# A convolutional attention block with a mixture of experts: z stored in partition order, its tables laid out ahead, and k's spreading transfers issued by SyncE

## The reference

```python
xn = ln_over_channels(x)                       # eps 1e-6
for s in (0, 2):                               # SHIFTS: once plain, once rolled by (-2, -2)
    xs = roll(xn, -s)
    for half in (xs[:, :32], xs[:, 32:]):      # 8 heads of 4 channels, windows of 4x4 pixels
        q, k, v = split(qkv_w @ half)          # qkv_w is 96 x 32
        lepe = depthwise_conv3x3(v, lepe_w)
        o = softmax(q @ k.T * 4 ** -0.5 + bias) @ v + lepe    # inside each window
    result += roll(o, s)
x = x + result
t = tokens(x)                                  # 9216 tokens of 64 for each image
tn = ln(t)                                     # eps 1e-5
p = softmax(tn @ router_w + router_b)          # 8 experts, the best 2 are kept and renormalised
t = t + sum_over_best_2(p_e * (tn @ expert_w[e] + expert_b[e]))
```

## Time and profile before

| | us |
|---|---|
| median of three runs | 3744.56 |
| lowest and highest run | 3741.43, 3759.62 |
| time of the profiled execution | 3730.37 |
| its span, first to last instruction | 3728.5 |

### The profile page before, as it was taken

One profiled execution on the slowest core, in us unless ns is written; L12 is line 12 of the kernel. 1 busy time (PEld: TensorE's weight loads), 2 busy tenths in 40 slices (PEclk: granted clock), 3 DMA queues, 4 the chain that ended last, 5 costly groups with the idle time before them and its releaser, 6 DMA issues.

```text
span 3728.5 us, 203806 instructions
## 1 busy us (share of the span) xinstructions
PE 3199.5 (86%) x82757; PEld 1956.7 (52%) x82757; DVE 3190.4 (86%) x6174; ACT 2233.5 (60%) x4514; POOL 2942.7 (79%) x5385
## 2 busy tenths in 40 slices
PE   3889989988898888898889888888889888989884
PEld 1655555555555555555555555555555555555541
DVE  2789989998999989998889988888889988889983
ACT  2676666666666656665566656665556666666640
POOL 3988878888888878887788878877788878788860
PEclk8999999999999999999899999999899989999996
DMA  1245455555455545555545555545455545455545
GB/s 27 60 97 126 117 123 121 129 120 122 118 127 121 124 109 129 115 127 115 120 110 127 122 117 121 125 111 122 113 120 125 124 115 123 114 116 126 125 104 126
DMA packets 415302, 432.05 MB, mean 116 GB/s; under 512 B 129984, under 2 KB 395888, under 8 KB 414320
## 3 DMA queue, kind: packets, MB, share of 16 engines
q1 hardware_dynamic: 248432, 304.94, 36.0%
q0 software_dynamic: 165888, 113.57, 12.9%
HBM read 245.79 MB, written 58.98 MB: 82 GB/s over the span
## 4 chain that ended last, share of the span: by engine, by line
PE 36%; SPq 23%; issue 15%; DVE 14%; DMA 5%; ACT 3%; POOL 2%; DVEq 0%; ACTq 0%; POOLq 0%
SPq L397 13%; PE bank L628 8%; PE bank L564 7%; DVE lepe L899 4%; SPq L429 4%; PE bank L549 3%; PE bank L641 3%; PE bank L584 2%; SPq L455 2%; DVE gx L887 2%; PE bank L633 2%; DMA gate_rows<-gateT 2%; DVE row_max L907 2%; DMA z<-fin 2%; PE bank L653 2%
## 5 line engine op out<-in xcount | busy, mean ns | idle before, releaser
L504 POOL DMA_DIRECT2D vx<-vt x3072 | 1561.7, 517 | 414.1 <-PE bank L633 403.3
L628 PEld LDWEIGHTS bank<-probT,vx 128*32 128x32 f32 x36864 | 824.6, 189 | 464.5 <-issue 452.8
L628 PE MATMUL bank<-probT,vx 128*32 128x16 f32 x36864 | 886.3, 234 | 159.2 <-issue 144.0
L493 POOL DMA_DIRECT2D kx<-k_sb x1536 | 741.0, 489 | 229.5 <-issue 102.8
L564 PEld LDWEIGHTS bank<-kx,qx 32*32 32x32 f32 x36864 | 584.9, 110 | 443.6 <-issue 441.3
L564 PE MATMUL bank<-kx,qx 32*32 32x64 f32 x36864 | 689.3, 223 | 133.3 <-issue 111.1
L899 DVE SCALAR_TENSOR_TENSOR lepe<-vpad,lepe_sb,lepe 128x384 f32<-128x384 f32 x960 | 673.5, 702 | 0.8 <-issue 0.8
L718 ACT ACTIVATE prob<-prob 128x512 f32<-128x512 f32 x576 | 367.4, 638 | 288.1 <-DVE prob L912 285.0
L887 DVE TENSOR_TENSOR gx<-gate_wide,yn_pair 128x768 f32<-128x768 f32 x384 | 397.4, 1036 | 112.9 <-PE bank L549 62.1
L523 POOL TENSOR_TENSOR lepe_p<-lepe_p,tap_sb 128x384 f32<-128x384 f32 x384 | 434.9, 1133 | 32.7 <-issue 11.3
L912 DVE TENSOR_TENSOR prob<-bank,row_max 128x512 f32<-128x512 f32 x576 | 398.4, 692 | 16.7
(11 more groups left out here) (87 smaller groups left out, 4517.8 us busy)
## 6 DMA issues: line engine op xcount, KB each, us to landing
gate_wide<-gate_rows SPq DMA_DIRECT2D x384, 384.0 KB
vx<-vt POOLq DMA_DIRECT2D x3072, 12.0 KB
kx<-k_sb POOLq DMA_DIRECT2D x1536, 24.0 KB
yn_pair<-yn POOLq DMA_DIRECT2D x384, 96.0 KB
z<-fin SPq DMA_DIRECT2D x1344, 24.0 KB
xs<-in_x SPq DMA_DIRECT2D x96, 192.0 KB
xt<-in_x SPq DMA_DIRECT2D x192, 96.0 KB
z0t<-z SPq DMA_DIRECT2D x192, 96.0 KB
```

Source lines behind the costliest of these rows:

```text
L493: pool.dma_start(kx[to + m:to + C:4, r % 2, m, :], k_sb[at + m:at + C:4, r % 2, :])\
L504: pool.dma_start(vx[to:to + TOK, r % 2, g * 8 + x:g * 8 + 8:2, odd, :], vt[at:at + TOK, r % 2, x::2, :, :].rearrange("p h n k -> p h (n k)"))\
L628: last = MM(bank_o[32 * c:32 * c + 32, at * TOK:(at + 1) * TOK], vx[:, kr % 2, :, at % 2, at // 2 * 4 + c], probT[:, kr % 2, at, c * TOK:( ...
```

## The change

- `z` has one row for each partition of `fin` in place of two images in channel order, so that a strip is stored by one transfer of 128 rows in place of 11. `load_tile` takes the order apart again: its z part has 8 transfers in place of 5, with rows in runs of 16. The columns of the weights are permuted to match (`product` reads them through `ba`), x is given a second time with its channels in the tile's order, and the output's channels are put back on the host.
- All weights, the bias and the constants come as one table laid out ahead, loaded by one transfer. The 56 loads of before and the copies by which DVE, PE and ACT formed the tables are gone.
- `spread_gates` issues two transfers for each product p, in the slots 4, 5, 0 and 1 of a tile, each with a semaphore of its own; before it was four transfers for all p at once.
- `spread_k` moves from POOL to SP.

```diff
-    take_logits=34, gates=36, gap_exp=37, turn_gates=38, pair_yn=38, store_gates=39, spread_gates=41,
+    take_logits=34, gates=36, gap_exp=37, turn_gates=38, pair_yn=38, store_gates=39, spread_gates=40,
...
+            sp.dma_start(table[:, :], tables).then_inc(table_loaded, 16)
...
             load_pair(0, 0)
+            sp.wait_ge(spread_cleared, N_SPREAD_CLEARED)
...
+                if st := s.strip("spread_k"):
+                    k, r = st
+                    wait_alone(sp, k_saved, k + 1)
+                    if s.later(r, 2):
+                        wait_alone(sp, score_made, (k - 1) * UNITS)
+                    for m in range(4):
+                        for at, to in ((0, C), (C, 0)):
+                            sp.dma_start(kx[to + m:to + C:4, r % 2, m, :], k_sb[at + m:at + C:4, r % 2, :])\
+                                .then_inc(k_spread[r % 2], 16)
...
-                    def put(roll, a, b, q0, q1, part):
-                        sp.dma_start(z_cols[roll][im][:, a, b, q0:q1, :, here]
-                                     .rearrange("b q y n -> q y (b n)"), fin[part:part + 2 * (q1 - q0), r % 2, :])\
-                            .then_inc(z_stored[r % 2], 16)
...
+                    sp.dma_start(z[bass.ds(s.image(r, STRIPS), 1)][:, :, here].rearrange("b c n -> c (b n)"),
+                                 fin[:, r % 2, :]).then_inc(z_stored[r % 2], 16)
...
+                    def put_z(dst, half, roll, c_to, c_from, n, at, row, rows):
+                        part = half * C + c_to * TOK
+                        sp.dma_start(dst[part:part + n * TOK, r % 2, at * W:(at + rows) * W],
+                                     z_of[roll][:, c_from:c_from + n, :, row * W:(row + rows) * W]
+                                     .rearrange("b c q n -> c q (b n)")).then_inc(tile_loaded[r % 2], 16)
+
+                    def put_rolled(half, at, row, rows):
+                        put_z(z2t, half, 1, 1, 0, 3, at, row, rows)
+                        put_z(z2t, half, 1, 0, 3, 1, at, row, rows)
                     for half in range(2):
+                        put_x(half)
+                        put_z(z0t, half, 0, 0, 0, 4, 0, t * (2 * SP) + half * SP, SP)
+
+                    put_rolled(0, 0, (t * (2 * SP) + H - ROLL) % H, ROLL)
+                    put_rolled(0, ROLL, t * (2 * SP), SP - ROLL)
+                    put_rolled(1, 0, t * (2 * SP) + SP - ROLL, SP)
...
-                if ti := s.tile("spread_gates"):
-                    k, r = ti
-                    wait_alone(sp, gate_stored[r % 2], (k // 2 + 1) * 16)
+                if (ti := s.in_tile("spread_gates")) and ti[2] < PAIRS:
+
+                    k, r, p = ti
+                    if p == 0:
+                        wait_alone(sp, gate_stored[r % 2], (k // 2 + 1) * 16)
                     if s.later(r, 1):
-                        wait_alone(sp, gx_made, k * PAIRS)
-                    by_expert = gate_rows[r % 2].rearrange("(f p e) n -> e f p n", f=2, e=2)
+                        wait_alone(sp, gx_made, (k - 1) * PAIRS + p + 1)
+                    by_expert = gate_rows[r % 2].rearrange("(f p e) n -> e p f n", f=2, e=2)
                     for odd in range(2):
-                        for half in range(2):
-                            sp.dma_start(gate_wide[odd * C:(odd + 1) * C, :, half, :],
-                                         by_expert[odd, half].unsqueeze(0).broadcast_to([C, PAIRS, SPX]))\
-                                .then_inc(gate_spread[r % 2], 16)
+                        sp.dma_start(gate_wide[odd * C:(odd + 1) * C, p, :, :],
+                                     by_expert[odd, p].unsqueeze(0).broadcast_to([C, 2, SPX]))\
+                            .then_inc(gate_spread[p], 16)
...
+                    dve.wait_ge(gate_spread[p], (k + 1) * (GATE_DMAS * 16))
                     if p == 0:
-                        dve.wait_ge(gate_spread[r % 2], (k // 2 + 1) * (GATE_DMAS * 16))
                         dve.wait_ge(yn_paired[r % 2], (k // 2 + 1) * 64)
```

More of the change, by code:

```diff
@@ new lines, in tile_channels, with lay_tables, put @@
+def tile_channels():
+    return [half * CH + h * HEADS + c * 2 + y for c in range(4) for h in range(HD) for half in range(2) for y in range(2)]
+def lay_tables(qkv_w, lepe_w, bias_table, router_w, router_b, expert_w, expert_b):
+    t = np.zeros((128, TABLE_COLS), np.float32)
+    def put(name, rows, col, value):
+        at, n = TABLE_AT[name]
+        t[:, at:at + n][rows, col] = value
+    for name, a in CONSTS.items():
+        put(name, slice(0, 128), slice(0, a.shape[1]), a)
+    for g in range(4):
+        roll, half = g // 2, g % 2
+        rows = slice(g * CH, (g + 1) * CH)
+        for h in range(HD):
+            for m in range(HEADS):
+                a, b, y = m // 4, m // 2 % 2, m % 2
+                for part, name in ((0, "wq"), (1, "wk")):
+                    put(name, rows, g * CH + a * 16 + h * 4 + m % 4, qkv_w[part * CH + h * HEADS + m])
+                here = (h - 1) % HD if roll and a and b else h
+                one = qkv_w[2 * CH + here * HEADS + m]
+                put("wv", rows, g * CH + h * 8 + y * 4 + b * 2 + a, one)
+                at = (a * 2 + b) * CH + roll * 16 + h * 4 + half * 2 + y
+                put("wo", rows, at, one)
+                put("taps", at, slice(0, 9), lepe_w[here * HEADS + m].reshape(9))
+    for g in range(4):
+        for a in range(2):
+            for i in range(TOK):
+                for m in range(4):
+                    for j in range(TOK):
+                        dr, dw = i // SP - j // SP + SP - 1, i % SP - j % SP + SP - 1
+                        put("bias", g * CH + a * TOK + i, m * TOK + j, bias_table[dr * (2 * SP - 1) + dw, a * 4 + m])
+    order = tile_channels()
+    for half in range(2):
+        rows = slice(half * C, (half + 1) * C)
+        put("router", rows, slice(half * E, (half + 1) * E), router_w[order])
+        for p in range(E // 2):
+            put("experts", rows, slice(p * C, (p + 1) * C), expert_w[2 * p + half][np.ix_(order, order)])
+        put("expert_bias", slice(half * E, (half + 1) * E), slice(half * C, (half + 1) * C), expert_b[:, order])
+        put("router_bias", slice(half * E, (half + 1) * E), 0, router_b)
+    return t
@@ L179, in metaformer_block @@
+def metaformer_block(nc, x, x_tile, tables, out):
     ctx = ExitStack()
@@ L321, in _ @@
         def _(sp):
[L322 to L341, removed]
-                for half in range(2):
[L343 to L354, removed]
-                        .then_inc(const_loaded, 16)
-                    sp.dma_start(ebias_sb[half * E:(half + 1) * E, rows], expert_b).then_inc(const_loaded, 16)
```

194 lines of the change are left out of this document (65 added, 129 removed).

## The result

The changed kernel took **3989.91 us** (median of four runs, 3981.11 to 3993.32). The kernel before, on the same chip, took 3742.99 (3718.65 to 3759.62). The ratio is 1.0662, 95% interval 1.06 to 1.0723: slower by 6.6%. The forecast was 3783 with a range up to 3930, so the time lies outside it. The profiled execution took 3992.08, its span is 3990.3.

The account below looks back on a forecast made before the run. Three close limits bound the kernel: SP, DVE and PE. A loop through the gates of p = 3 (38.35 us a tile against 37.46) adds 80 us, less 42 for setup: +38 on the median, 3783 us, range 3570 to 3930.

Parts of the forecast that it names:

- start and tail: Outside the tile loop: earlier first matmul saves 34 us, last tiles no longer waiting for four gate spreads 8 more.
- k's price: Each SBUF-to-SBUF k issue on SP taken at 0.64 us; eight transfers 5.2 us, ends 3.2 to 7.0.
- x issue to gates in use: From the first x load to gates of p = 3 landed, queued behind x on two engines: 9.55 us, 9.0 to 10.5.
- z's loads on four and three engines: New z loads would crowd few engines, leaving up to 2.5 us ahead of gates and k: 40.8 us a tile.
- The range for x's start: On SP's queue, x loads start 17.05 us after `fin`, 13.1 to 20.4 with all ends.
- The forecast's own case: Loop through the gates of p = 3 gives 37.5 to 39.5 us a tile, 3706 to 3886 us; chance 0.42.
- Engines or issues dearer: k issues at 0.88 us or z loads crowding few engines: up to 41 us a tile, 3950 to 4020; chance 0.15.
- Cheap issues: k transfers on SP cost 0.40 us with gap: tile 36.35 us, total 3603 us; chance 0.22.
- the loop never closes: Loads at 5.9 us, z landing in 2.2: gates of p = 3 don't delay DVE, 3550 us; chance 0.13.
- Nothing but the setup: PE and DVE pace all tiles at 37.5 us; only the 42 us are saved, 3703 us; chance 0.08.
- The pace of PE and DVE alone: If the gates' loop stays open, DVE and PE set the tile at 35.5 to 36 us; chance 0.13.
- The forecast's turning point: Gates of p = 3 arriving 26.2 us after `fin`: there the loop eats the 42 us saved elsewhere.

Follow-up runs that it names:

- e2: Changed kernel with the gates of p = 3 issued ahead of the k transfers and x loads, k still on SP: 3718.77 us, 0.9947 of the kernel before.
- e4: Changed kernel with all eight gate transfers in slot 5 of a tile, k still on SP: 3668.44 us, 0.9821 of the kernel before.
- e1: Changed kernel with k's eight transfers back on POOL, all else as changed: 3632.79 us, 0.9712 of the kernel before.
- e6: Changed kernel with k's transfers back on POOL and the gates of p = 3 issued ahead of the x loads: 3422.87 us, 0.9151 of the kernel before.
- e3: Changed kernel with the 62-row x loads split into 48 and 14 rows, two issues more: 3874.69 us, 1.0367 of the kernel before.
- e5: Changed kernel with z's rows interleaved by roll, stored by eight transfers of 16 rows in place of one: 4233.69 us, 1.1318 of the kernel before.
- e10: Changed kernel with four of k's eight transfers on SP and four on POOL: 3834.26 us, 1.0247 of the kernel before.
- b1: Kernel before with k's transfers moved to SP and nothing else changed: 4417.9 us, 1.1828 of the kernel before.

## Why the prediction was wrong

**The mechanism was right.** The profile has what the prediction named: a loop of one tile from `fin` over z's landing, SP's queue and the gates of p = 3 back to `fin`; a DVE wait once a tile at p = 3; SP waiting for `fin` with throughput to spare (479.1 us in 99 times); PE's share of the chain gone. 28.95 + 12.15 = 41.1 us of loop (medians) stand against the measured tile of 41.32. The two experiments that take the gates of p = 3 out of the queue (e2, e4) end DVE's wait, and the one that takes k out (e1) shortens it. The two other causes that were named before those runs fell with them: if k's own lateness were the cost, e2, where k is later, would have been slower than 3990; and had the lower granted clock been a cause of its own, none of the three was expected to move. What part the clock has in the product's way to the next `fin` (12.15 us, 11.32 in e6) was not separated.

**The step that failed is the length of that loop**, forecast 26.6 + 11.75 = 38.35. Its terms, forecast and measured (from the timelines of the changed kernel; means over 66 tiles, since means add up, here to the tile of 41.32 within 0.01):

```
term                              forecast  measured  difference
fin to the first tile load          3.0       2.66      -0.3
ten tile loads                      7.45      7.61      +0.2
gates of p = 2                      1.4       1.87      +0.5
eight k transfers                   5.2       6.18      +1.0
x issue to gates p = 3 in use       9.55     10.74      +1.2
product p = 3 to the next fin      11.75     12.26      +0.5
```

The whole way from `fin` to the product is 29.07, +2.5, with +0.5 behind it; the tile itself is 2.97 longer than forecast. The two terms that failed most are the way from x's issue to the gates in use and the price of k. Between the first and the last tile this made +319.4 us where +80 were forecast, 239 too few; start and tail gave 57.6 in place of 42. The sum against the profiled execution thus missed by 224 us (3992 against 3768). Against the medians it is 207, since the profiled execution of before lay 14 us under its median and that of after 2 above.

- *k's price.* A single issue on SP takes a median of 0.589 us, within the 0.64 that was taken:

```profile
L391 SPq DMA_DIRECT2D kx<-k_sb x1536: 486/589/1921, 23.1 to 3873.0; - x192
```

From the first k to the first x it is 6.07, so 0.76 a transfer. The 0.64 came from three issues in a row in the setup, when nothing else ran. Longer single issues (up to 1.9; one of 1.32 in the tile shown) and the semaphore instructions ahead of the x loads are in the 0.76.
- *x issue to gates in use* was the term least known: it was built from shares of engines, with ends of 9.0 and 10.5, and measured just above the upper. e3 shows that its largest part, the wait behind x's 62-row loads on two engines, was right in kind: 3.3 of the 6.3 us of landing go when x is divided otherwise. Its parts were not right: x was to have landed 1.5 + 5.25 = 6.75 us after its issue and the gates 2.3 + 0.5 behind it; by the updates x lands after 9.7 and the gates 0.9 later. The 5.25 came from the start of the program, where nothing else moved. The Trainium skill (DMA: Bandwidth & Descriptors, Why a DMA increments its semaphore by 16 and not by 1; the prediction names another section of that page) says that a transfer is divided over the largest number of engines up to 16 that divides the slowest dimension of both sides. The runs agree: a set of x loads makes 28 updates with 62 rows and 84 with 48 and 14, and the ten tile loads the 102 named under e5. These counts fit 2, 16, 14, 4 and 3 engines, if a transfer on fewer than 16 counts one update more.
- *z's loads on four and three engines*, the mechanism weighed against the trace, given up to 2.5 us: e5 puts it near 1.0. The forecast was right to leave it out: the transfers did run on so few engines, and it costs little, since 7.5 us of issue go by meanwhile. (The 5.4 us of that passage is 5.5 by its own numbers, 98 KB against 93 in 5.25.)
- *Errors that add up.* Five of six terms were too small and one too large by 0.3. The range for x's start, 13.1 to 20.4 (its terms as stated reach 3.0 + 8.4 + 1.4 + 7.0 = 19.8), held the median of 18.18; the one behind it, 9.0 to 10.5, missed by 0.2. But these ends were not carried to the total: even 19.8 + 10.5 + 11.75 make a tile of 42.05 us, and a time above 4100. The forecast's own case stopped at 39.5 a tile and its dearest rival at 41, with nothing in the text that excluded what lies beyond.

**The parts of the sum outside the loop.** The start gave 34.7 us to the first matmul (forecast 34), 41.4 to the first tile. The tail gave 16.2 where 8 were forecast.

**The rivals.** *Engines or issues dearer* (0.15, 3950 to 4020) holds the time, and a part of its reason: from one k issue to the next it takes 0.76, half way between the forecast's 0.65 and its 0.88. That is 1 us of the 2.97; z crowded nothing by much, and the rest is in terms that it did not name. *Cheap issues* and *the loop never closes* fell with the 6.07 and 7.49 us (medians) of k and the tile loads. *Nothing but the setup* fell with the tile of 41.32. *The pace of PE and DVE alone*, 35.5 to 36 us in the forecast, was seen in e6: it is 34.7. The forecast's turning point, gates 26.2 us after `fin`, lies near the runs in which those gates still hold DVE up: e1 at 24.8 is faster than before, e10 at 27.3 is slower.

**Which part of the change did what.** Between the kernels with k on POOL and with k on SP, the new layout, table and gate order are worth -107 us (e1 against before) and -428 (the changed kernel against b1). k's move costs 357. Before, SP's queue was one of three limits close together; the fewer stores took it away and the move put it back, in the form of latency instead of throughput. The chance of 0.46 on faster was too high: 0.35 of it lay in rivals that needed issues or loads cheaper than the rows that the text itself called the nearest.

## What to carry to other kernels

When an in-order queue stops being the throughput limit, look for the transfer in it that closes a loop with the engine that starts it, and add up everything issued between: here 28.95 us, in a queue that waited a fifth of the time (its five largest waits are 816 of 3990 us). In such a loop the order in the queue counts as well as the number of issues. Two transfers moved ahead (e2) gave back 271 us, against 357 for sixteen a tile taken out (e1), and together with k's transfers off that queue (e6) they make the kernel 8.5% faster than the one before.

Carry the ends of each term through to the total before choosing a range: errors of terms on one path add up, they don't average.

## What the runs showed of the hardware beyond what was expected

- One store of 128 rows is issued in 0.38 us and lets the first load go 2.18 us later; eight stores of 16 rows with the same bytes take 6.5 us for both (e5). The 4 us between them go with the number of transfers, not with the bytes.
- A transfer that someone waits for lands later behind others: the first load comes 2.18 us after z's store in the changed kernel, where SP had waited 4.9 us for `fin` on average and so issued nothing, 3.05 behind four gate spreads and two outputs (e2), 4.9 behind eight and two (e4). The gates' own 24 KB store landed in 2.2 us before and in 5.8 in the changed kernel (medians).
- Issue time taken out of a queue came back only in part: 6.3 us of issue less gave 4.1 us a tile (e1), since the x loads behind it landed 1.4 us later after their issue and the gates behind them 0.6.
- The granted TensorE clock was lower in the slower kernels: 0.923 before, 0.888 in the changed kernel, 0.962 in e6. How much time the clock costs by itself no run here shows. The same 82756 matmuls took 3294.7 us in the changed kernel and 3092.1 in e6. In the window 1633 to 1641 of the changed kernel, in which DVE stands for 5.67 us, the granted clock was 0.79 after 1.00 in the 3 us ahead of it, a mean of the full 2.4 GHz and the lower level of 1.2 (columns: window, its length, busy time of PE, PEld, DVE, ACT and POOL, clock, DMA share, GB/s):

```profile
1630.00:1633.00 3.00, 2.07 (x62) 1.42 (x58) 3.00 (x4) 2.11 (x6) 2.91 (x5) 1.00 0.82 203
1633.00:1641.00 8.00, 7.58 (x177) 4.50 (x181) 2.30 (x5) 3.48 (x7) 0.53 (x1) 0.79 0.47 121
```
